# Whole-array bias and offset products, and VectorE work moved to ScalarE or merged, in a six-layer decoder kernel

## The reference

```python
x = _layernorm(x + _L0_attn_ref(x, ...))    # A: 16 heads, window of 7; attn * conn / (sum + 1e-9); @ wo.T + bo
x = _layernorm(x + _L0_xattn_ref(x, ctx))   # B: cross attention, vp = v @ Wv.T + bv
x = _layernorm(x + _L0_ffn_ref(x, ...))     # X: 8 experts, each takes the 16 tokens with the largest sigmoid(x @ Wr.T)
x = _layernorm(x + _L1_attn_ref(x, ...))    # C: attention with a decay mask, qkv and output biases
x = _layernorm(x + _L1_xattn_ref(x, ctx))   # D, E: argmax picks one context row per token, then 16-head attention on it
x = _layernorm(x + _L1_ffn_ref(x, ...))     # F: 8-bit rows, ternary weights, depthwise conv of 3, silu, 8-bit rows

def act_quant(x):      # F, twice
    scale = 127.0 / jnp.clip(jnp.max(jnp.abs(x), axis=-1, keepdims=True), 1e-05)
    return jnp.clip(jnp.round(x * scale), -128, 127) / scale
def weight_quant(w):   # F, once per weight
    scale = 1.0 / jnp.clip(jnp.mean(jnp.abs(w)), 1e-05)
    return jnp.clip(jnp.round(w * scale), -1, 1) / scale
```

## Time and profile before

| | |
|---|---|
| device time, 3 runs | 1100.07, 1100.21, 1093.01 us (median 1100.07) |
| device time of the profiled execution | 1096.73 us |
| its span, first to last instruction | 1094.9 us |
| mean granted TensorE clock | 0.947 of 2.4 GHz |
| PE busy | 964.1 us (88% of the span) |
| DVE busy | 910.3 us (83%) |
| ACT busy | 752.5 us (69%) |
| POOL busy | 163.2 us (15%) |

### The profile page before, as it was taken

One profiled execution on the slowest core, in us unless ns is written; L12 is line 12 of the kernel. 1 busy time (PEld: TensorE's weight loads), 2 busy tenths in 40 slices (PEclk: granted clock), 3 DMA queues, 4 the chain that ended last, 5 costly groups with the idle time before them and its releaser, 6 DMA issues.

```text
span 1094.9 us, 19705 instructions
## 1 busy us (share of the span) xinstructions
PE 964.1 (88%) x7038; PEld 693.7 (63%) x7038; DVE 910.3 (83%) x2503; ACT 752.5 (69%) x1854; POOL 163.2 (15%) x401
## 2 busy tenths in 40 slices
PE   5758889999999999999999999999999998887552
PEld 4536557676767676767767776768676756564331
DVE  4798776689898989898989989898999877867754
ACT  2223454768696878778787878786969795867643
POOL 2000110111112020302021211112120301010000
PEclk9878899999999999999999999999999998988865
DMA  7823021211110302030303020120212001000000
GB/s 224 325 67 106 1 87 34 63 46 42 49 58 9 98 21 86 6 101 1 106 1 90 17 81 26 45 63 20 77 40 68 10 1 30 1 20 1 10 10 10
DMA packets 36626, 58.90 MB, mean 54 GB/s; under 512 B 6784, under 2 KB 15872, under 8 KB 36016
## 3 DMA queue, kind: packets, MB, share of 16 engines
q1 hardware_dynamic: 36528, 57.64, 16.7%
HBM read 28.65 MB, written 4.19 MB: 30 GB/s over the span
## 4 chain that ended last, share of the span: by engine, by line
PE 68%; ACT 14%; DVE 12%; POOL 3%; issue 3%; DMA 0%; SPq 0%; ACTq 0%; POOLq 0%; DVEq 0%
PE bank_c L450 20%; PE bank_a L450 11%; PE banks_e L450 7%; PE bank_f L450 5%; PE bank_x L450 5%; PE bank_x L644 4%; PE bank_a L542 3%; PE bank_c L472 2%; ACT squares_out L1362 2%; ACT area_e L1559 2%; DVE x L880 2%; DVE area_a L1046 2%; PE banks_e L788 1%; PE banks_e L801 1%; ACT area_bx L1350 1%
## 5 line engine op out<-in xcount | busy, mean ns | idle before, releaser
L1284 DVE SCALAR_TENSOR_TENSOR area_f<-area_f,w_convw 128x254 f32<-128x254 f32 x256 | 111.5, 477 | 6.0 <-ACT area_f L1588 4.9
L1350 ACT ACTIVATE area_bx<-bank_x 128x512 f32<-128x512 f32 (+1 forms) x144 | 70.0, 498 | 29.3 <-PE bank_x L644 10.4
L1208 DVE TENSOR_REDUCE neg_top<-banks_e 128x8 f32<-128x1024 f32 x64 | 76.1, 1211 | 10.4 <-PE banks_e L450 10.3
L996 DVE TENSOR_TENSOR area_a<-area_a 128x512 f32<-128x512 f32 x112 | 73.4, 681 | 8.6 <-ACT area_a L1350 8.5
L1588 ACT ACTIVATE area_f<-area_f,w_convb,w_convw 128x256 f32<-128x256 f32 x128 | 69.6, 594 | 13.7 <-DVE area_f L1275 13.6
L1350 ACT ACTIVATE area_a<-bank_a 128x512 f32<-128x512 f32 (+1 forms) x80 | 44.1, 551 | 49.9 <-PE bank_a L450 28.3
L1350 ACT ACTIVATE area_bx<-bank_c 128x512 f32<-128x512 f32 x64 | 34.8, 544 | 61.3 <-PE bank_c L450 41.3
L1046 DVE TENSOR_TENSOR area_a<-area_a 128x512 f32<-128x512 f32 x112 | 74.4, 681 | 0.4
L1559 ACT ACTIVATE area_e<-banks_e 128x512 f32<-128x512 f32 x128 | 67.9, 599 | 1.3 <-PE banks_e L801 1.0
L1050 DVE TENSOR_TENSOR area_a<-area_a 128x512 f32<-128x512 f32 x96 | 65.1, 679 | 0.1
L1350 ACT ACTIVATE area_e<-banks_e 128x512 f32<-128x512 f32 (+1 forms) x80 | 45.8, 593 | 16.1 <-PE banks_e L472 5.9
(11 more groups left out here) (314 smaller groups left out, 2682.7 us busy)
## 6 DMA issues: line engine op xcount, KB each, us to landing
area_a<-area_a SPq DMA_DIRECT2D x96, 224.0 KB
area_a<-in_xT SPq DMA_DIRECT2D x16, 256.0 KB, 2.9
x<-in_x SPq DMA_DIRECT2D x16, 256.0 KB, 3.0
area_bx<-in_ctxT SPq DMA_DIRECT2D x16, 256.0 KB, 2.8
area_d<-in_ctxT SPq DMA_DIRECT2D x16, 256.0 KB, 3.0
y<-x SPq DMA_DIRECT2D x16, 256.0 KB, 2.2
w_wqkv_e<-in_wqkv_e SPq DMA_DIRECT2D x1, 3072.0 KB, 10.5
area_f<-in_raw SPq DMA_DIRECT2D x2, 1024.0 KB, 11.4
```

Source lines behind the costliest of these rows:

```text
L996: return dve.tensor_tensor(product_of(wi).rearrange("p (n t) -> p n t", t=P), qT0.rearrange("p c (b t) -> p (c b) t", t=P), kT0.rearrange( ...
L1208: dve.tensor_reduce(top[:, b, :, r:r + 2, 0].rearrange("p (par c) r -> p r c par", c=DC), banks_e[:, r:r + 2, :].rearrange("p r (c par k) ...
L1284: last = dve.scalar_tensor_tensor(c4[:, i, :, dst], h4[:, i, :, src], cwt3[:, 2 * jj + i, k:k + 1], c4[:, i, :, dst], ALU.mult, ALU.add)
L1350: return act.activation(dst, src, ACT.Copy)
```

## The change

1. Width of the small products. `bias_parts` becomes three 128-row tiles, zero outside their three rows, and `w2_sums` and `offset` become 128 rows; L462 and L861 then use all 128 rows. `w2_sums` is now a VectorE reduction over `w2q` (sum in each row, 128 rows of it), in place of eight PE products with ones.
2. Setup: the ternary weights are made by ACT (absolute values with a sum, scale plus `MAGIC`, `Sign` of the difference), in 4 slices; DVE's setup is cut into many small steps.
3. A: the two sums and the 1e-9 term become two multiplications by `conn` and `conn + 1e-9` and one sum. X: the reciprocal of 64 x 128 sigmoid denominators goes; their bits are flipped so that the order is reversed, and the reciprocal is taken on 128 x 16 after the transposition. E: two multiplications become one of twice the size.
4. D: `chosen_key` is written by ACT, ahead of `chosen_v`. F: the 8-bit rounding of the rows goes to ACT; its subtraction of `MAGIC` rides in a copy that was there already; one tiny operation fewer in either half of F; `scale_rows` no longer waits for the rounding.
5. The order tables of all engines are new.

```diff
-SLICES = 8
+SLICES = 4
...
     "POOL": (
-        "ABABXABXCABCXEABCXEAFBCXEAFBCXEAFBCXEAFBCEXAFBCXEAFBCXEAFBCXEAFBCXEAFBCXEAFBCXEAFBCXEFCEXFCEFEFF"
+        "ABABXABXCABCXEABCEXAFBCXEAFBCXEAFBCXEAFBCXEAFBCXEAFBCXEAFBCXEAFBCXEAFBCXEAFBCXEAFBCXEFCEXFCEFEFF"
...
             def project_rows(bank, weights, actT, bias=None):
                 if bias is not None:
-
-                    row = slice(32 * bias, 32 * bias + 3)
-                    pe.matmul(bank[:, :], ones_bf[row, :], bc(bias_parts[row, :], 1, GB), start=True, stop=False)
+                    pe.matmul(bank[:, :], ones_bf[:, :], bc(bias_parts[bias][:, :], 1, GB), start=True, stop=False)
...
-                pe.wait_ge(setup_pool, 10)
-                pe.wait_ge(setup_dve, 12)
-                mm(bank_f[0:32, 0:D], [(ones_f16[:, :], w2q[:, j, :]) for j in range(HJ)]).then_inc(setup_pe, 1)
-                yield
...
-                    n = DC * HID // SLICES
-                    for k in range(SLICES):
-                        part = raw[:, k * n:(k + 1) * n]
-                        m = own.mark(dve.tensor_scalar(part, part, small[:, 2 + i:3 + i], MAGIC, ALU.mult, ALU.add))
-                        dve.wait_ge(own.sem, m)
-                        m = own.mark(dve.tensor_scalar(part, part, MAGIC, 1.0, ALU.subtract, ALU.min))
-                        dve.wait_ge(own.sem, m)
-                        last = dve.tensor_scalar(q[:, k * n:(k + 1) * n], part, -1.0, None, ALU.max)
...
+                m = own.mark(dve.tensor_reduce(bias_rest, w2q[:, :, :].rearrange("p j n -> p n j"), X, ALU.add))
...
-                m = own.mark(dve.tensor_reduce(den1, e_head, X, ALU.add))
...
+                weighted = own.mark(dve.tensor_tensor(terms, e_rows, bc(conn_more[:, :], 1, GB), ALU.mult))
+                yield
+                own.mark(dve.tensor_tensor(e_rows, e_rows, bc(conn[:, :], 1, GB), ALU.mult))
+                yield
+                dve.wait_ge(own.sem, weighted)
+                m = own.mark(dve.tensor_reduce(mx, terms_a.rearrange("p (b w h) -> p b h w", b=GB, w=WIN), X, ALU.add))
...
-                m = own.mark(dve.reciprocal(sig, sig))
...
+                m = own.mark(dve.tensor_scalar(r2.bitcast(U32), sig.bitcast(U32), 0x7FFFFFFF, None, ALU.bitwise_xor))
...
-                key = chosen_key[g % 2]
-                dve.tensor_tensor(key[:, 0], bc(bank_c[:, 0:P], 1, 2), bc(w["parity"][:, :], 2, P), ALU.mult)
-                dve.tensor_tensor(key[:, 1], bc(bank_c[:, P:2 * P], 1, 2), bc(w["parity"][:, :], 2, P),
-                                  ALU.mult).then_inc(d_key_out, 1)
...
-                for b in range(GB):
-                    m = own.mark(dve.tensor_scalar(xq_f[:, b * D:(b + 1) * D], x[:, b, :], sc1_f[:, b:b + 1], MAGIC,
-                                                   ALU.mult, ALU.add))
-                yield
-                dve.wait_ge(own.sem, m)
-                for b in range(GB):
-                    last = dve.tensor_scalar(xq_f[:, b * D:(b + 1) * D], xq_f[:, b * D:(b + 1) * D], MAGIC, None, ALU.subtract)
-                last.then_inc(f_scaled, 1)
...
+                    act.activation(q, raw, ACT.Abs, accum_out=small[:, i:i + 1]).then_inc(setup_act, 1)
...
+                            made[k] = own.mark(act.activation(part, part, ACT.Copy, scale=small[:, 2 + i:3 + i], bias=MAGIC))
...
+                            last = act.activation(q[:, (k - 1) * n:k * n], raw[:, (k - 1) * n:k * n], ACT.Sign,
+                                                  bias=less_magic)
...
-                act.wait_ge(d_key_out, g + 1)
+                act.wait_ge(d_v, g + 1)
+                for par in range(2):
+                    act.activation(chosen_key[i][:, :, par, :], blocks(bank_c[:, 0:T], GB), ACT.Copy,
+                                   scale=w["parity"][:, par:par + 1])
+                    yield
...
+                act.wait_ge(f_scaled, 2 * g + 1)
+                for b in range(GB):
+                    last = act.activation(xq_f[:, b * D:(b + 1) * D], xs[g % NX][:, b, :], ACT.Copy, scale=sc1_f[:, b:b + 1], bias=MAGIC)
+                last.then_inc(f_quantized, 1)
...
-                copy(xqT_f, bank_f[:, :]).then_inc(f_xqT_out, 1)
+                act.activation(xqT_f, bank_f[:, :], ACT.Copy, bias=-MAGIC).then_inc(f_xqT_out, 1)
```

More of the change, by code:

```diff
@@ L194, in build @@
         ones_bf = sb("ones_bf", [P, P], BF16)
[L195 to L196 removed]
+        bias_parts = [sb(f"bias_parts{i}", [P, D], BF16) for i in range(3)]
+        conn, conn_more = sb("conn", [P, WH]), sb("conn_more", [P, WH])
         decay = sb("decay", [P, P])
@@ L892, in split_bias @@
                     m = own.mark(dve.tensor_tensor(rest, rest, bias_round[r, :], ALU.subtract))
+                yield
                 dve.wait_ge(own.sem, m)
-                return dve.tensor_copy(parts, part)
+                dve.wait_ge(setup_pool, 12)
+                for at in range(r.start, r.stop, 32):
+                    last = dve.tensor_copy(bias_parts[at // 32][at:at + 32, :], bias_rest[at:at + 32, :])
+                last.then_inc(setup_dve, 1)
+                yield
             def setup(_):
@@ L1402, in setup @@
                 yield
-                act.wait_ge(setup_pe, 9)
-                copy(w2_sums[:, :], bank_f[0:1, 0:D]).then_inc(setup_act, 1)
-                yield
+                for i, (raw, q) in enumerate(((raw1, w1q[:, :, :].rearrange("p c n -> p (c n)")),
+                                              (raw2, w2q[:, :, :].rearrange("p c n -> p (c n)")))):
+                    act.wait_ge((raw1_in, raw2_in)[i], 16)
+                    act.activation(q, raw, ACT.Abs, accum_out=small[:, i:i + 1]).then_inc(setup_act, 1)
+                    yield
+                    act.wait_ge(setup_dve, 10 + i)
+                    act.wait_ge(setup_act, 9 + 2 * i)
+                    act.wait_ge(setup_pool, 11)
+                    n, made = DC * HID // SLICES, {}
+                    for k in range(SLICES + 1):
+                        if k < SLICES:
+                            part = raw[:, k * n:(k + 1) * n]
+                            made[k] = own.mark(act.activation(part, part, ACT.Copy, scale=small[:, 2 + i:3 + i], bias=MAGIC))
+                            yield
+                        if k:
+                            act.wait_ge(own.sem, made[k - 1])
+                            last = act.activation(q[:, (k - 1) * n:k * n], raw[:, (k - 1) * n:k * n], ACT.Sign,
+                                                  bias=less_magic)
+                            if k == SLICES:
+                                last.then_inc(setup_act, 1)
+                            yield
             def windowed(g):
```

238 lines of the change are left out of this document (118 added, 120 removed).

## The result

The changed kernel takes **1112.12 us** (median of 4 runs, 1110.26 to 1117.42) against 1099.67 of the kernel before (4 runs): ratio 1.0136, 95% interval 1.010 to 1.0171. The forecast was 1076. The profiled execution took 1111.07 us, its span is 1109.3.

What follows compares the result with a forecast made beforehand. PE was taken to bound the full pipeline, with DVE fullest in the filling and chain length counting in the drain. 15 + 4 + 1 + 2 = 22 us off 1096.73 gives 1074.7, given as 1076; range 1058 to 1092.

Steps and rivals of the forecast that it cites:

- step 2: Setup in the filling: work moves from DVE to ACT, which has room; gain of 4 us (-2 to 10).
- step 4: ACT takes parity copies and roundings, 1.9 us more per group, covered by 12 us idle per period; no cost.
- step 1: PE's bias and offset products on 128 rows: the holes around them go, gaining 15 us.
- Rival A: Holes come from the bank's hand-over or a semaphore wait, not the width: 1090 us, 10%.
- DVE per group: Stations A, X, D, E, F: DVE some 3.6 us lighter of 53 per period; worth 1 us (0 to 5).
- rival D: PE's waits for ACT grow by 0.5 to 1 us per period and eat 6 to 11 us: 1085, 14%.
- Rival C: ACT's hand-overs become the bound: later `d_v_out` holds up PE's `bank_c` products, 40 us lost: 1115, 4%.
- The drain: Last group's `scale_rows` no longer waits for DVE's rounding at L1266: gain of 2 us (0.5 to 5).

Runs made afterwards that it cites:

- e8: e4 with the sum over w2q made by PE products and a copy on ACT instead of the DVE reduction: 1095.4 us, ratio 0.9976.
- e14: e4 with DVE's sum over w2q in four pieces of 64 columns, other steps between them: 1096.3 us, ratio 0.9983.
- e10: e6 plus D's keys moved to ACT: 1087.5 us, ratio 0.9884.
- e3: Kernel before plus the width and all moves per group, keeping its setup and order tables: 1092.0 us, ratio 0.9953.
- e4: All operations of the changed kernel, walked by the order tables of the kernel before: 1101.0 us, ratio 1.0017.
- e9: e6 with F's rounding kept on DVE in half the instructions, the subtraction riding in ACT's copy: 1081.6 us, ratio 0.9833.
- e11: e6 plus F's rounding moved to ACT: 1085.5 us, ratio 0.9873.
- e1: Kernel before with the 128-row width of bias and offset products alone, no order touched: 1087.1 us, ratio 0.9890.
- e5: Changed kernel with SP's order table alone put back to that of the kernel before: 1115.5 us, ratio 1.0138.
- e6: e1 plus the three merges on DVE (A's sums, X's reciprocal, E's multiplication): 1082.9 us, ratio 0.9868.

## Why the prediction was wrong

In ratios: the width -0.0110, the merges -0.0022, the moves to ACT +0.0085, the setup's move +0.0064, the tables +0.0119; the sum is the +0.0136 measured. So the forecast failed in three places: step 2, forecast as a gain of 4 us, cost 7; step 4, put at nothing, cost 9; the new tables, put at nothing, cost 13. One by one:

1. **Tile width: right, size nearly.** Forecast 15 us, measured 12 to 13.5. Every hole went where step 1 said, and the next weights now load while the bias product streams, as it said too. Of 1.1 us per group, 0.87 and 0.94 arrived per period. Rival A is out. The Trainium skill (TensorEngine Tiling, "Key Properties") says that a change of tiling mode drains the engine. The trace before and after at the same place agrees: 0.20 to 0.30 us went with each narrow product.

2. **The setup leaves DVE: the step that failed first.** Forecast a gain of 4 (bounds -2 and 10), measured a loss of 7. ACT's terms were sized well: the slices took 0.71 us each and the 2048-column operations 1.9, 15 us in all as taken. The work did leave DVE, and PE's wait of 1.60 us before group 3's `w_wq` did shrink (timeline of the changed kernel):

```profile
129.53 1.97 PE L451 MATMUL bank_a<-area_a,w_wq 128*128 128x256 f32 x8 [0.40 <-DVE x L878]
```

 What failed is the sentence "ACT is busy 46.3 of 110 us in the filling, so it has room even for 23". The chain of the filling passes through ACT's short copies again and again, and 5.6 us of the setup's operations, 0.6 to 1.9 us at a time, stand in it ahead of such copies, however idle the engine is on the mean. And the reduction over w2q, "again 2.3 us", took 3.69 (timeline), at a place where the chain went through DVE:

```profile
151.23 3.69 DVE L999 TENSOR_REDUCE area_s<-w2q 128x256 f32<-128x2048 f16 x1
```

 How the 7 us divide between ACT's operations and this reduction stays open (e8 and e14).

3. **DVE per group: right.** Forecast 1 us (0 to 5), measured 2.4, not certain. DVE went from 53 to 51.0 us per 58 (I had said 49; the period is longer than forecast, so this share holds less than a group's work).

4. **ACT per group: the step that failed next.** I costed it at nothing, with "ACT's 12 us of idle time per period" as the cover, and left the mechanism to rival D (6 to 11 us, 14%). 9 us came, the size of rival D, but only 4.2 of them in the ten periods, 0.4 us per period where D said 0.5 to 1; the rest came in the filling and the drain. Rival C had the place (from 300 to 880 us PE's waits for `chosen_v` are 2.3 us in e10, e3 and e4, 0.6 before) but not the price of 40. The Trainium skill's advice is to leave additions and multiplications to VectorE (ScalarE: Activation LUTs, "Rules for kernel authors"). The traces agree for the operation itself: a parity copy of 256 columns took 0.466 us on ACT, 0.424 on DVE. I set the advice aside since only the engine's room seemed to count. Keeping the rounding on DVE at half the instructions (e9) has the lowest median, though not certainly a lower one than e11.

5. **The drain: wrong.** The 4.75 us wait of the earlier trace rows was not on the chain. In the chain of the kernel before ACT's copy of the scales starts at 1056.73 us, directly behind group 14's norm on ACT, and so does e1's; DVE's rounding, done by 1055.8, was hidden behind that norm. Moved to ACT the rounding came into the chain (0.80 us in e11, e3 and the changed kernel). So the forecast 2 us were not to be had. The changed kernel's PE waits there nearly as long as before, now for the tiny DVE product that makes `rs1`:

```profile
1070.54 0.43 PE L818 MATMUL bank_f<-w_ident,area_f 128*128 128x128 f32 x2 [4.41 <-DVE area_f L1251]
```

6. **The tables: not costed at all.** The forecast put them at nothing without a reason; what it says of the order is that PE's products around the bias product stay as they were. It warned of the filling and the drain only; the cost, 13 us, the largest single loss, came for the most part in the full pipeline (10.1 us in ten periods), where PE's standing grew from 18.5 to 26.5 us in 580 with the same operations. It is spread over many small waits, and which engine's table carries it stays open: only SP's was exchanged alone (e5, no gain). The only rival that ended slower was C; the tables, which touch every engine's every step, should have been a second, with a price per period.

That the changed kernel's 1112 us lie next to rival C's 1115 is chance: from 300 to 880 us its PE has no visible wait for `chosen_v` at all.

## What to carry to other kernels

Where a small product of 3 rows or 1 row stands in the stream of a busy PE, widen it to 128 rows: here that took nothing from the stream (0.22 us for 512 columns) and saved the pauses around it. The products that stay on 32 rows or 32 columns in both kernels were not tried. Judge a move between engines by the chain, not by busy shares: ACT was 42% busy in the filling, and its new operations of 0.6 to 1.9 us still stood in the chain. Whether pieces with others' steps in between do better than one long instruction is open. And cost a new schedule as an edit of its own: run the new operations under the old order before searching a new one.

## What the runs showed of the hardware

The scatter of one and the same kernel goes with PE's granted clock. 73 runs of the kernel before lie between 1093.15 and 1105.90 us; their mean granted clock is 0.952 for the four fastest and 0.938 for the slowest, the correlation is -0.88, and a fitted line gives 7.2 us per 0.01. e9's six runs do the same: 1075.66 us at 0.954, 1085.17 at 0.945. The clock falls below 1.00 only in the filling and in the drain, where PE idles more. Windows of the drain, e6 (clock 0.950 over its run) and then e9 (0.943):

```profile
960.00:1020.00 60.00, 41.32 (x318) 27.63 (x312) 46.43 (x111) 40.44 (x89) 4.53 (x12) 0.89 0.03 10
```

```profile
960.00:1020.00 60.00, 43.79 (x298) 29.32 (x296) 41.39 (x97) 37.61 (x83) 4.40 (x12) 0.80 0.03 10
```

From 300 to 880 us the clock is 1.00 in every profiled execution. This fits the columns: the ten periods agree within half a microsecond and the other two don't; e9's profiled drain is 5.6 us longer than e6's, though its median is the lower.

A reduction of 2048 half-precision values per row, to 256 sums of 8 values that lie 256 apart, took 3.69 us on VectorE, where one of 2048 adjacent float32 values to a single sum takes 2.26. Whether the stride or the number of sums makes it was not tried.
